# The same instructions in another order: step tables and PSUM banks of a two-layer decoder laid anew

## What is computed

```python
x = _layernorm(x + _L0_attn_ref(x, ...))       # state space scan, 16 states
x = _layernorm(x + _L0_xattn_ref(x, ctx_512, ...))
x = _layernorm(x + _L0_ffn_ref(x, ...))        # 8 experts, top 2, and a shared one
x = _layernorm(x + _L1_attn_ref(x, ...))       # gated scan
x = _layernorm(x + _L1_xattn_ref(ctx_512, x, ...))   # top 76 of 256 by row
x = _layernorm(x + _L1_ffn_ref(x, ...))        # 8 experts, top 2, and a shared one
```

## Time and profile before

| | |
|---|---|
| median of 3 runs | 572.75 us (572.34 to 572.91) |
| the profiled execution | 574.76 us, span 573.0 us |
| mean granted TensorE clock | 0.939 |
| TensorE busy | 509.6 us, 89% |
| VectorE busy | 468.0 us, 82% |
| ScalarE busy | 400.1 us, 70% |
| GpSimd busy | 304.6 us, 53% |

### The profile page before, as it was taken

The page is one execution under the profiler, slowest core; times in us unless marked ns, Lnnn a source line. Parts: engine busy times, 40 slices in busy tenths (PEclk is TensorE's granted clock), DMA queues, the critical chain, the costliest instruction groups (busy, mean ns, idle before and its releaser), DMA issues.

```text
span 573.0 us, 8810 instructions
## 1 busy us (share of the span) xinstructions
PE 509.6 (89%) x2416; PEld 371.4 (65%) x2416; DVE 468.0 (82%) x1053; ACT 400.1 (70%) x941; POOL 304.6 (53%) x466
## 2 busy tenths in 40 slices
PE   3676668788769999999999999999899999999996
PEld 2444456556556686677676687675777667787664
DVE  1269998899999999999999999899788976575351
ACT  2398598789888986889769996878878662362221
POOL 1058775188757771777454974765657533213221
PEclk9795578799988999999999999999899999999999
DMA  7494000044703525135505350447046313537000
GB/s 207 159 341 190 1 0 3 26 150 150 234 1 101 173 92 185 47 85 170 174 0 150 88 142 15 127 128 220 0 127 170 106 51 104 187 95 220 2 9 10
DMA packets 29824, 63.60 MB, mean 111 GB/s; under 512 B 4752, under 2 KB 8592, under 8 KB 29392
## 3 DMA queue, kind: packets, MB, share of 16 engines
q1 hardware_dynamic: 29776, 63.04, 36.1%
HBM read 61.91 MB, written 1.11 MB: 110 GB/s over the span
## 4 chain that ended last, share of the span: by engine, by line
PE 59%; DVE 17%; ACT 11%; issue 8%; POOL 3%; DMA 1%; DVEq 0%; SPq 0%; POOLq 0%; ACTq 0%
PE work L621 34%; PE work L678 11%; PE h_bank L597 6%; DVE acc L1208 5%; PE work L597 4%; ACT dA L975 4%; DVE st L1192 3%; POOL dbu L549 2%; ACT L844 2%; DVE wk L1159 1%; DVE m L1155 1%; ACT L975 1%; PE h_bank L701 1%; DVE row L1034 1%; DVE bst L1027 1%
## 5 line engine op out<-in xcount | busy, mean ns | idle before, releaser
L549 POOL TENSOR_TENSOR dbu<-du,b_rows 128x512 f32<-128x512 f32 x128 | 163.2, 1276 | 27.3 <-DVE du L1144 20.5
L975 ACT ACTIVATE dA<-dts,a_neg 128x127 f32<-128x127 f32 x512 | 156.4, 355 | 17.7 <-DVE st L1192 16.8
L1192 DVE TENSOR_TENSOR_SCAN st<-dA,dbu 128x512 f32<-128x512 f32 x128 | 155.2, 1215 | 2.9 <-ACT dA L975 2.3
L621 PE MATMUL work<-stream,xsT 128*128 128x352 f32 (+1 forms) x320 | 109.3, 474 | 2.2 <-ACT xsT L844 0.9
L597 PE MATMUL h_bank<-ident,st 128*128 128x128 f32 x512 | 85.9, 301 | 23.9 <-DVE acc L1208 17.1
L1208 DVE SCALAR_TENSOR_TENSOR acc<-h_bank,c_cols,acc 128x512 f32<-128x512 f32 x128 | 93.3, 729 | 5.6 <-PE h_bank L597 3.2
L597 PEld LDWEIGHTS h_bank<-ident,st 128*128 128x128 f32 x512 | 66.3, 155 | 47.2 <-DVE st L1192 31.5
L572 POOL TENSOR_TENSOR h_tok<-h_tok,wf 128x352 f32<-128x352 f32 (+1 forms) x48 | 41.7, 871 | 81.1 <-ACT h_tok L844 47.6
L621 PEld LDWEIGHTS work<-stream,xsT 128*128 128x128 f32 x320 | 58.4, 195 | 28.4 <-issue 2.5
L494 POOL TENSOR_SCALAR var<-mv 128x1 f32<-128x1 f32 x56 | 13.1, 234 | 87.5 <-DVE mv L1028 87.1
L678 PE MATMUL work<-stream,h_t 128*128 128x256 f32 x224 | 53.2, 381 | 0.0
(11 more groups left out here) (159 smaller groups left out, 816.7 us busy)
## 6 DMA issues: line engine op xcount, KB each, us to landing
stream<-in_stream SPq DMA_DIRECT2D x72, 352.0 KB, 3.5
stream<-in_stream SPq DMA_DIRECT2D x32, 384.0 KB, 3.7
b_rows<-b_dram SPq DMA_DIRECT2D x32, 256.0 KB, 5.8
stream<-in_stream SPq DMA_DIRECT2D x8, 360.0 KB, 3.8
stream<-in_stream SPq DMA_DIRECT2D x8, 256.0 KB, 3.6
wg<-in_wg SPq DMA_DIRECT2D x1, 1280.0 KB, 8.6
wu<-in_wu SPq DMA_DIRECT2D x1, 1280.0 KB, 11.1
wd<-in_wd SPq DMA_DIRECT2D x1, 1280.0 KB, 13.6
```

What stands on the lines that cost most here:

```text
L549: gp.tensor_tensor(tile, du[:, batch % 2, :, lo:hi], b_rows[:, b % 2, k:k + 1, :].to_broadcast([P, ET, P]), ALU.mult).then_inc(s["dbu_read ...
L621: last = mm(t[:, col:col + width], lhs(c), rhs(c), start=(c == 0), stop=(c == depth - 1))
L975: last = A(dA[i % DA_RING][:, t, 1:P], dts[:, batch % 2, t, lo + 1:hi], ACT.Exp, scale=a_neg[:, t, k:k + 1])
L1192: V.tensor_tensor_scan(st[:, i % ST_RING].rearrange("p t l -> p (t l)"), dA[i % DA_RING].rearrange("p t l -> p (t l)"), dbu[:, i % DBU_RIN ...
```

## The change

The change replaces the strings of `ORDER` for all five engines and `BANK`. Nothing else differs. All steps and their instructions are the same; only the order of the steps on each engine, the bank of each result, and what follows from the order (table loads) differ. A line or two of it:

```diff
 ORDER = {
     "pe": [
-        "ppppppppmsmpassssssssssasssssssssssmmsmssssmmppssmspsspppsssffsmmmmpsssffffffffffppssspsfmmmmssffsfsfffsfmmsff",
+        "ppppppppmasssspsssssssssssasmssssssssmmssmsssppmmssmspsmmmmsppppfsffffssfssffffffssmmmppssfspsmsffffsffsfsffsf",
...
 BANK = [
-    "01230123012013213021302301201323012302302310101230121031023020130212310230132130313202031201302120301301233103",
+    "01230123012013203120231203110112032102121032102103213023012301230132001301301030210132013010132013201021301230202",
```

More of the change, by code:

```diff
@@ new lines @@
+        "hhghffgghgsmmmfsgmfffsfgfffgfhhfsfffssffaaaaaaaaaaaaammassfapsfmffffggfggsmmmmggghhhhmshshssgffgghhgfggsssgggm",
+        "mggffffffmggsfssgggaaaaaaaaaaaaaasgfsgafsggsfsfsffffgfmmffssffsmsfsssmmmmhhhhghhggssffmmmsffffgfssmfsfffffhhfs",
+        "fffsfffsfsfggfgfssmmgmmmmmssggghhhhsghhggsgsgssggffgfgsssmsmmffffmfshhfffmmfsfmffssffsfffmmmmffssggfgfggghhhhs",
+        "ghhsggssffgfffffsgfhhggsggffgmmmggfgmgggffmmfmfffgfffffffgggffgghhhhfhgghgffffgfffffhhffaaaaaaaaaaaaaffffffffg",
+        "gfgfggghhhhhhgggghhggggggggggggggggggggggppsmmmfhhhg",
@@ new lines @@
+        "sggmsgggaasahhhhffmmmmmffsfasffgggggahfffshmagsfffsfffashaaaahmmsamggsfffffffaamfsggasgamhhhhsggsshahgggshffsh",
+        "ffafgggggsagmmmmmsggaffggassagsggssfffsmsgggfffaaafffsssssfffffffsmmfmssmsmhhhhsffsffsfmmmmmsffgggggshfffhsfff",
+        "ghsfffhssggmsfffffffsmmmggfssgmggssmgggshhhhmmmassssgggggffsffsmmfffhsmhsfffmmhsfffmssfffghssfffffffafggmsggms",
+        "gshhhhffggffsfgggshhffhshmmmggggggggfffmmmgggammmffffffmaaamfffffffaggfagggffaafffahhhhffggggggfffhhaffffffhhg",
+        "gffffffffggghhhhgghhggghhggggggggggggggggggggggppppp",
@@ new lines @@
+        "gghsffffggshmmmggsfhhfffffffssaaaaaaaaaaasffffffsaaasffammmpsffffggggppmmsgmmmghhhhmhggghssssffffhhggsgsggsggf",
+        "fggggmmfffffsssgaaaaaaaaaaagfgggssaaasggffsasgffffsssffsggmmmffffssssshhhhmmmmmhhsffffmmmsggsfffffshhsffsffffs",
+        "fffsffsggggffffssgmmmsgsmmmmmhhhhgggshggghggsssssffffggsssfmmmhhffffssfffffmmmfsffssfffmmssffffggggmmmssghhhhg",
+        "ggghsggffffhsfffffghhggffggfggggmmmggffmmmffffmmffgggffffgggffffhhhhgghaaaaaaaaaaagghfffffffhhfffffffffffffggg",
+        "ggghhhhhhggghhgggggggggggggggggggggggssaammfffhhhggg",
@@ L131 @@
+        "ffssspsssssssffffffffffmmmmmmmmmsssffffffsffshhhhhsggggggggfffhfffshhsssmmffffffffffsmmmggggggsssssggmmshhhhhs",
+        "ssssffffffffshmmmmmmfffgggggggghmmmhfffssssssffffffffffmmggggggsggsffffffffhhhhhhhhfffggggggggmmmmmmggggggfffm",
+        "mmggmmffffffffffffffffffggggggggfffhhhhhhhfffhffffffffffgggggggghhhhhhhhggggggggggggggggggggggggssaaaaaaaaaaaa",
         "aaaaaaaaaaaaaaaaaaaaaaaaaaaaaaaaaaaaaaaaaaaaaaaamfhg",
@@ L133 @@
     "sp": [
-        "lllclllcccbcrrlbccrccbxcwccccccccrccccccccrccccwcbcccwrcccccwcccccocccrccccccccoccccccccccccccccccccocrcwccccc",
-        "ccccccccccccocwccccocccccccccccccccccccccooo",
+        "lllllcclcbcrrclcbrccxcccwbccccccrccwrccccccccccccrccccccwcccccbocccccccwcccccoccrcccccccwccccccccccccoccrccccc",
+        "ccccccccccccoccwcocccccccccccccccccccccccooo",
     ],
```

41 lines of the change are left out of this document (12 added, 29 removed).

## The result

| | before | changed |
|---|---|---|
| median | 572.55 us (571.31 to 572.91, 4 runs) | 563.62 us (562.46 to 564.15, 4 runs) |
| profiled execution | 574.76 us, span 573.0 | 562.46 us, span 560.6 |
| mean granted TensorE clock | 0.939 | 0.949 |

The ratio is 0.9845, 95% interval 0.9824 to 0.9867: 8.9 us faster. The forecast was 569.5 us, the range 565.0 to 575.5. The sign was right; the size was not, and the range missed it by 1.4 us.

What follows compares the result with a forecast made beforehand. VectorE was taken to bound the early part, TensorE the late part, with both nearly full between. Terms -4.3 + 1.0 = -3.3 us on a 572.75 us median gave 569.5 us, range 565.0 to 575.5.

Steps and rivals of the forecast that it cites:

- What bounds the kernel: VectorE bounds 40 to 76 us, TensorE 420 to 560; both nearly full from 201 to 313, TensorE idling 1.8 us.
- The stretch at 410 us: TensorE's wait at ones,sq for ScalarE and the clock fall behind it go: -1.8 - 2.5 = -4.3 us.
- The clock's share: Near 410 us, four groups taking 7.47 us would cost 5.0 at full clock, so the clock cost 2.5 us.
- The rule weighed against the rows: Skill page charges half of throttled time: 35 us overall, about 17 in the first stretch; counted only where TensorE bounds.
- T3 of unit 1: TensorE step near 201 us: new 2.8 us wait for VectorE's product, partly absorbed by 1.8 us idle: +1.0 us.
- it comes to T3 at 201.4 + 5.0 = 206.4: TensorE's arrival with 5.0 us more work ahead; VectorE's product expected at 209.2 us, hence a 2.8 us wait.
- The rival built on that wait: Clock falls behind the new 2.8 us wait near 201 us, delaying VectorE too: +2.2 us, 575.0 us; chance 0.24.
- The two long waits: TensorE's waits for VectorE's row, up to 157.3 and 172.1 us: taken 0, ends -1 and +1 us.
- the first unit: Half of batch 1's in-projection moves between second and third turn: taken 0, ends 0 and +1.2 us.
- The fast rival: VectorE's 4.2 us of waits from 40 to 172 us disappear, everything behind starts earlier: 565.3 us; chance 0.10.
- Table loads 74: ScalarE has four table loads fewer, 5.1 us, hidden by its idle time: taken 0, ends -1 and 0.
- banks 0: Newly laid PSUM banks may make a claim wait for another reader: taken 0, ends -0.5 and +0.5 us.

Runs made afterwards that it cites:

- tail_405: Order of the kernel before up to 405 us, then the changed kernel's order on all engines and its PSUM banks; 567.62 us, ratio 0.9918.
- sq_first: Kernel before with sq of unit 4 moved on ScalarE alone, ahead of the skip copy, table load and dA; 572.91 us, ratio 1.0020.
- act_first: Kernel before with only ScalarE's order near 410 us changed: sq, its dA, normalization, xsT and three output steps moved earlier; 570.06 us, ratio 0.9976.
- after_again: The changed kernel unaltered, measured once more; 564.08 us, ratio 0.9843 to the kernel before.
- gram_again: Changed kernel with TensorE's kv product of unit 0 moved behind unit 1's skip turn, second measurement; 559.70 us, ratio 0.9792 to the kernel before.
- tail_new: Order of the kernel before up to 188 us, then the changed kernel's order; 572.51 us, ratio 1.0007.
- hybrids: Kernels with one kernel's order (before or changed) on all engines up to a time and the other's behind it; several cuts, each measured separately.

## Why the prediction missed

- **What bounds the kernel: right for the ends, too coarse for the middle.** "Behind it TensorE has a fixed amount of work to do, and every microsecond that it idles or runs at half clock after that lands in the time": the loss says the same. But I treated the part from 201 to about 400 us as having 1.8 us of idle time and nothing else to gain. It held a loss of 8.4 us between the marks, more than half of it (5.0 us) in delays of 0.03 to 0.3 us that no wait row names.
- **The stretch at 410 us, -4.3 us: right.** `ones,sq` has no idle time, the clock is 1.00, and tail_405 has -4.4 us of median and -4.7 of loss. The clock's share was put too low: busy over count made 5.0 us of what takes 4.25 us at full clock, so half clock cost 3.2 us and not 2.5. My reason, that TensorE has something to do meanwhile, holds; the runs add that ScalarE's order alone doesn't do it (sq_first 0, act_first 1.8 us of loss), since two readers and `dA` of unit 7 compete there.
- **The rule weighed against the rows.** The rule of the Trainium skill, "TensorE: Matmul & The Clock Gate", section "HAM oscillation — how this bites in real kernels", half of the throttled time, gives as an estimate 3.4 us for the 6.8 us at half clock near 410 us; the rows give 3.2. Where TensorE is the bound the trace so agrees with it. For the first stretch the estimate by the same rule is 17 us, and there no run bears it out. The clock there rose from 0.53 to 0.64 in the change, VectorE set the pace in both, and the early part won nothing. No run tried that stretch at full clock, so what it would bring isn't measured.
- **T3 of unit 1, +1.0 us: wrong.** VectorE's part of the sum was near: from act_first, which has before's order and no late start, the product ends at 196.8, plus 9.1 is 205.9, and in after_again it ends at 205.4. The failed term is "it comes to T3 at 201.4 + 5.0 = 206.4". From act_first that is 198.1 + 5.0 = 203.1, but after_again has it at 205.6, 2.5 us later, and with no idle time. In the measure of the loss it is 3.2 us late there (87.4 against 84.2 us): 1.4 us stand ahead of turn 56, where half clock lasts longer, and the other 1.8 behind it, most of them in two new waits for ScalarE. after_again:

```profile
190.08 1.45 PE L621 MATMUL work<-stream,xsT 128*128 128x352 f32 x4 [0.53 <-ACT h_t L844]
195.77 1.45 PE L621 MATMUL work<-stream,xsT 128*128 128x352 f32 x4 [0.64 <-ACT gram L844]
205.60 0.49 PE L597 MATMUL work<-ident,h_tok 128*128 128x128 f32 x3
```

  A TensorE that is late doesn't wait. The rival built on that wait (575.0) fell with it.
- **The two long waits, the first unit, taken 0.** The first part as a whole came out within its ends: about 0. But in it the change has a new wait of VectorE that gram_again shows to cost some 3 us. I had placed the danger at the in-projection, with an end of +1.2; the step was the `kv` product a little further on, 2.07 us at half clock.
- **The fast rival (565.3) had nearly the right number for the wrong cause.** Its 4.2 us of early VectorE waits became 3.0 us; the gain came later.
- **The failed step in one sentence:** everything between T3 and 400 us was taken as unchanged but for 1.8 us, a term put at nothing that was worth 5.2 us, and T3's +1.0 us didn't come. The runs have -5.2 - 4.7 = -9.9 us of loss behind mark 1 and, by the means, +1.1 us ahead of it: -8.8 us, with -8.9 measured.
- **Table loads 74, banks 0:** four loads fewer, no effect seen. That a bank can hold a product 2.2 us was shown in before's order (sq_first); the bank table wasn't tried by itself.

**What stays open.** Of the 5.2 us of the middle, the two `adj` steps account for 0.6 to 1.1 (up to 1.5 with what happens behind mark 2). The other 4 us belong to the order behind 188 us as a whole (tail_new) and to no step that was tried; the other five steps of VectorE that left the middle were not moved alone, and that fewer of them is the cause is a guess. Nor is it known what share of hybrids' misses is the seam's banks and what its order.

## What to carry to other kernels

Where two engines are both some 95% full, count what work stands in the stretch and whether it could stand elsewhere: deferrable steps of the fuller engine (here the neighbour search) belong where that engine has pauses. Before a sum is made, measure each stretch between two fixed instructions by idle time plus half clock, taken from the starts of the matmuls, not by the longest waits; and read the same stretch in a second execution before taking a difference of 2 to 4 us in an early part as the change's. A wait cured on one engine's order should be followed to the next claim of its result's PSUM bank and to the work pushed back.

## What the runs showed of the hardware that I had not expected

- With the same order, a part of 150 to 180 us repeats to 0.1 us: the middle has 159.0 to 159.1 in six kernels and 152.6 to 152.7 in five, and the last part 178.5 to 178.6 in six, though they reach mark 2 at 378.9 to 391.4 us. The spread of executions sits mostly in the first 230 us, with starts of the first scans at 36.6 to 39.5 us, and in how long half clock lasts there: 0.72 against 0.53 in the same window of the same kernel. Near 410 us half clock lasts 6.8 us in most kernels with the order of before and 3.4 us in two.
- A fall of the clock is cheap or dear by where it is. In the stretch from 40 to 76 us the clock was 0.53 before and 0.64 in the change, and the first part is no shorter for it; 6.8 us at half clock near 410 us cost 3.2 us of a loss of 4.7 us.
